# The opening of a graph-network kernel: first input tile in halves, third tile normalised by VectorE, edges turned last, biases fetched first

## The reference

```python
h = jnp.maximum(_layernorm(x, axis=-1), 0.0)
x = x + _L0_gnn_ref(h, edge_index, edge_type_5, ...)   # two chained projections, masked attention of 16 heads, output projection
h = jnp.maximum(_layernorm(x, axis=-1), 0.0)
x = x + _L1_gnn_ref(h, edge_index, edge_type_8, ...)   # mean over the edges of each of 8 relations, then a gate
h = jnp.maximum(_layernorm(x, axis=-1), 0.0)
x = x + _L2_gnn_ref(h, src, dst, ...)                  # two layers of neighbour means
h = jnp.maximum(_layernorm(x, axis=-1), 0.0)
x = x + _L3_gnn_ref(h, edge_weight, ...)               # a sparse weight built from the edges
```

## Time and profile before

| what | value |
|---|---|
| median of 3 runs | 928.15 us (927.82 to 928.22) |
| the profiled execution's own time | 927.87 us |
| its span in the profile | 926.1 us |
| PE busy | 906.8 us, 98% of the span |
| DVE, ACT, POOL busy | 611.5, 359.2, 492.3 us |
| mean granted TensorE clock | 0.996 of full speed |

### The profile page before, as it was taken

How to read it: one execution, slowest core, us unless ns; L and a number is a source line. 1 busy time by engine, 2 the same in 40 slices (tenths; PEclk the granted TensorE clock), 3 DMA queues, 4 the chain that set the end, 5 groups by cost and what they waited for, 6 DMA issues and landing times.

```text
span 926.1 us, 13755 instructions
## 1 busy us (share of the span) xinstructions
PE 906.8 (98%) x4787; PEld 799.0 (86%) x4787; DVE 611.5 (66%) x993; ACT 359.2 (39%) x558; POOL 492.3 (53%) x436
## 2 busy tenths in 40 slices
PE   4999999999999999999999999999999999999998
PEld 4999999998888888888888888888888878888886
DVE  6998888896996735665656565565656565434545
ACT  6433333345885343223223223232325235224422
POOL 5334446775765515757657575756686402220463
PEclk8999999999999999999999999999999999999999
DMA  8998756634336644344554444444333534323412
GB/s 207 241 277 224 229 155 151 167 85 119 53 52 204 178 155 146 92 151 114 152 152 130 153 113 150 113 148 111 97 91 137 182 98 154 114 93 91 140 42 91
DMA packets 89907, 128.60 MB, mean 139 GB/s; under 512 B 34480, under 2 KB 67456, under 8 KB 89856
## 3 DMA queue, kind: packets, MB, share of 16 engines
q1 hardware_dynamic: 72784, 123.54, 43.8%
q0 software_dynamic: 15552, 0.11, 4.0%
q10 hardware_dynamic: 1520, 4.30, 1.4%
HBM read 117.17 MB, written 7.59 MB: 135 GB/s over the span
## 4 chain that ended last, share of the span: by engine, by line
PE 90%; DVE 3%; ACT 2%; POOL 1%; DMA 1%; issue 1%; POOLq 0%; DVEq 0%; ACTq 0%
PE ps L682 49%; PE ps L476 17%; PE ps L756 9%; PE ps L520 4%; PE ps L645 4%; PE ps L600 2%; PE ps L543 2%; PE ps L556 2%; DMA weight_d<-weight_sum,cell 1%; PE ps L435 1%; POOL weight_d L1890 1%; PE ps L892 1%; DVE wlo_all L1388 1%; POOL mean_lo L1869 0%; PE ps L443 0%
## 5 line engine op out<-in xcount | busy, mean ns | idle before, releaser
L1388 DVE TENSOR_TENSOR wlo_all<-raw,whi_all 128x1024 fp32r<-128x1024 f32 x120 | 200.4, 1681 | 119.6 <-ACT whi_all L972 118.5
L476 PE MATMUL ps<-acts,whi_all 128*128 128x384 f32 (+1 forms) x640 | 164.1, 337 | 0.8 <-DVE acts L1400 0.6
L1869 POOL TENSOR_TENSOR mean_lo<-mean_f,mean_hi 128x384 fp32r<-128x384 f32 x76 | 88.3, 1162 | 120.4 <-ACT mean_hi L1124 120.4
L1124 ACT ACTIVATE mean_hi<-mean_f 128x384 fp32r<-128x384 f32 x76 | 39.9, 525 | 277.2 <-DVE mean_f L1562 277.2
L682 PE MATMUL ps<-whi_all,mean_hi 128*128 128x512 f32 x452 | 139.5, 390 | 0.3 <-POOL mean_lo L1869 0.3
L682 PE MATMUL ps<-wlo_all,mean_hi 128*128 128x512 f32 x452 | 139.3, 389 | 0.0
L682 PE MATMUL ps<-whi_all,mean_lo 128*128 128x512 f32 x452 | 139.3, 389 | 0.0
L972 ACT ACTIVATE whi_all<-raw 128x1024 fp32r<-128x1024 f32 x120 | 125.1, 1050 | 32.0 <-PE ps L682 28.5
L476 PEld LDWEIGHTS ps<-acts,whi_all 128*128 128x128 f32 x640 | 116.8, 190 | 1.2 <-DVE acts L1400 0.9
L1890 POOL DMA_INDIRECT weight_d<-weight_sum,cell x48 | 95.5, 1989 | 30.4 <-DMA weight_d<-weight_sum,cell 17.5
L476 PE MATMUL ps<-acts,wlo_all 128*128 128x384 f32 (+1 forms) x320 | 107.6, 336 | 0.0
(11 more groups left out here) (211 smaller groups left out, 1705.6 us busy)
## 6 DMA issues: line engine op xcount, KB each, us to landing
raw<-in_L_gnn_weight SPq DMA_DIRECT2D x64, 512.0 KB
rows_b<-rows_d SPq DMA_DIRECT2D x24, 384.0 KB, 4.8
raw<-in_L_gnn_w_gate SPq DMA_DIRECT2D x16, 512.0 KB
raw<-in_L_gnn_W_self SPq DMA_DIRECT2D x16, 512.0 KB
raw<-in_L_gnn_W_neigh SPq DMA_DIRECT2D x16, 512.0 KB
count_d<-total_r SPq DMA_DIRECT2D x8, 576.0 KB
rel_r<-count_d SPq DMA_DIRECT2D x8, 576.0 KB, 4.5
raw<-in_L_gnn_wq SPq DMA_DIRECT2D x32, 128.0 KB
```

Source lines behind the costliest of these rows:

```text
L476: mm = pe.matmul(ps[:, j % 2, 0:N], stationary[j % RING][:, k, :], acts[:, a, moving, k, :], start=i == 0, stop=i == 3 * KT - 1)
L1124: act.activation(mean_of(q, k, 0)[:, 0, :], sums_of(q, k), ACT.Copy).then_inc(S["mean_hi"], 1)
L1388: dve.tensor_tensor(wlo_row[slot], raw[slot][:, :], whi_row[slot].bitcast(F32), ALU.subtract)\
L1869: pool.tensor_tensor(mean_of(q, k, 1)[:, 0, :], sums_of(q, k), mean_of(q, k, 0)[:, 0, :].bitcast(F32), ALU.subtract).then_inc(S["mean_lo"], 1)
```

## The change

It changes the lists of the opening and nothing behind them.

- SP fetches tile 0 of x in two halves of columns, each with a semaphore, so there is one more DMA ahead of everything else of SP.
- DVE takes the statistics by halves: half 0 of tile 1 now stands before the reciprocal and shift of tile 0, and half 0 of tile 2 before those of tile 1. The edge keys are formed after tile 0 and wait for two of the four edge fetches; the types and the third key come after `start_low(0)`.
- The reciprocal and shift of tile 2 come behind `turn_tile(0, 0)`. DVE then normalises the third tile in two halves (`start_norm`, a multiplication and an addition, with no maximum). ACT takes the maximum while it writes the high part (Relu in place of Copy), DVE while it writes the low part.
- The edges are turned behind all four pieces of x, into other columns of the same bank as the biases. PE no longer waits for their copy; ACT does, before it copies the biases. DVE copies the edges behind `start_low(3)`, and the three softplus operations follow there. Both stand before `turn_tile(0, 1)`.
- POOL fetches the biases right behind the identity, before its tables.

```diff
--- before.py
+++ after.py
@@ -164,7 +164,7 @@
         ps = ctx.enter_context(nc.psum_tensor("ps", [P, 8, 512], F32))
 
 
-        names = """x_in edges_in etw_in bcol_in brow_in out_stored
+        names = """x_in ends_in edges_in etw_in bcol_in brow_in out_stored
             rows_stored mask_based tables_zeroed weights_zeroed mask_in weight_in
             ident_made order_made spare_made zeros_made ones_made mask_base_made
             key_made edge_rows edges_turned edge_cols edges_moved met_made rows_free
@@ -189,6 +189,7 @@
         weights_added = [sem(f"weights_added{q}") for q in range(GROUP)]
         rel_in = [sem(f"rel_in{i}") for i in range(2)]
         x_part = [sem(f"x_part{nt}") for nt in range(NT)]
+        x_half = sem("x_half")
         v_staged = [sem(f"v_staged_{s}") for s in ("even", "odd")]
 
 
@@ -276,7 +277,9 @@
         @block.sync
         def _(sp_):
             x_rows = x.rearrange("(t p) d -> p t d", p=P)
-            for nt in range(NT):
+            sp_.dma_start(xres[:, 0, 0:HALF], x_rows[:, 0, 0:HALF]).then_inc(x_half, 16)
+            sp_.dma_start(xres[:, 0, HALF:D], x_rows[:, 0, HALF:D]).then_inc(x_part[0], 16)
+            for nt in range(1, NT):
                 sp_.dma_start(xres[:, nt, :], x_rows[:, nt, :]).then_inc(x_part[nt], 16)
 
             def key_rows(s):
@@ -423,7 +426,7 @@
             def turn_edges():
                 pe.wait_ge(S["edge_rows"], 1)
                 for f in range(4):
-                    mm = pe.transpose(ps[:, 0, EC * f:EC * f + EC], e_row[:, f, :], ident[0:EC, 0:EC])
+                    mm = pe.transpose(ps[:, 2, P + EC * f:P + EC * f + EC], e_row[:, f, :], ident[0:EC, 0:EC])
                 mm.then_inc(S["edges_turned"], 1)
 
             def turn_two(y, source, f):
@@ -481,17 +484,15 @@
 
             pe.wait_ge(S["ident_made"], 2)
             for n, (nt, k0, k1) in enumerate(START):
-                if n == 2:
-                    turn_edges()
                 pe.wait_ge(S["h_ready"], n + 1)
                 for k in range(k0, k1):
                     mm = pe.transpose(ps[:, 2 + 2 * nt + k // 4, P * (k % 4):P * (k % 4) + P],
                                       h0[:, nt, P * k:P * k + P], ident[:, :])
                 mm.then_inc(S["start_turned"], 1)
+            pe.wait_ge(S["start_lo"], 1)
+            turn_edges()
             pe.wait_ge(S["bcol_in"], 16 * 6)
-            pe.wait_ge(S["start_lo"], 1)
             pe.transpose(ps[:, 2, 0:6 * KT], b_in[:, :], ident[0:6 * KT, 0:6 * KT]).then_inc(S["bcol_made"], 1)
-            pe.wait_ge(S["edge_cols"], 1)
 
             def turned_at(k):
 
@@ -900,7 +901,8 @@
         @block.scalar
         def _(act):
             for f, field in enumerate((src, dst, et8, et5)):
-                act.dma_start(e_in[:, f, :], field.rearrange("(c p) -> c p", p=P)).then_inc(S["edges_in"], 16)
+                act.dma_start(e_in[:, f, :], field.rearrange("(c p) -> c p", p=P))\
+                   .then_inc(S["ends_in" if f < 2 else "edges_in"], 16)
             act.wait_ge(S["ones_made"], 1)
             act.activation(std[:, 0, :], epsc[:, :], ACT.Sqrt).then_inc(S["ones_made"], 1)
             act.dma_start(etw_b[:, :], etw.partition_broadcast(P)).then_inc(S["etw_in"], 16)
@@ -938,8 +940,8 @@
 
                 nt, k0, k1 = START[n]
                 act.wait_ge(S["start_turned"], n + 1)
-                act.activation(acts[:, 0, 0, k0:k1, P * nt:P * nt + P], start_block(nt, k0, k1), ACT.Copy)\
-                   .then_inc(S["start_hi"], 1)
+                act.activation(acts[:, 0, 0, k0:k1, P * nt:P * nt + P], start_block(nt, k0, k1),
+                               ACT.Copy if nt < NT - 1 else ACT.Relu).then_inc(S["start_hi"], 1)
 
             HALVES = [slice(0, HALF), slice(HALF, D)]
 
@@ -980,10 +982,8 @@
             norm_relu_0(*START[0])
             norm_std(0, 1)
             norm_relu_0(*START[1])
+            norm_std(0, 2)
             start_high(0)
-            norm_std(0, 2)
-            norm_relu_0(*START[2])
-            norm_relu_0(*START[3])
             tile_high(0, 0)
             start_high(1)
             start_high(2)
@@ -995,6 +995,7 @@
             act.activation(sp[:, 4, :], sp[:, 3, :], ACT.Ln, bias=1.0).then_inc(S["sp_ln"], 1)
             act.activation(ones_r[:, :], same[:, 0, 0:P], ACT.Copy).then_inc(S["ones_made"], 1)
             act.wait_ge(S["bcol_made"], 1)
+            act.wait_ge(S["edge_cols"], 1)
             act.activation(bcol[:, :], ps[:, 2, 0:6 * KT], ACT.Copy).then_inc(S["bcol_made"], 1)
             act.wait_ge(S["bcol_made"], 2)
 
@@ -1276,28 +1277,44 @@
                 dve.tensor_scalar(shift[:, nt, :], mv[:, nt, 0:1], rstd[:, nt, :], -1.0, ALU.mult, ALU.mult)\
                    .then_inc(S["shift_ready"], 1)
 
-            def start_stats(nt):
-
-                dve.wait_ge(x_part[nt], 16)
-                norm_stats(0, nt)
-
-            for nt in range(NT):
-                start_stats(nt)
-                if nt < NT - 1:
-                    norm_shift(0, nt)
-            dve.wait_ge(S["edges_in"], 16 * 4)
-            dve.scalar_tensor_tensor(e_row[:, KEY, :], e_in[:, 0, :], float(N), e_in[:, 1, :], ALU.mult, ALU.add)\
-               .then_inc(S["key_made"], 1)
-            dve.scalar_tensor_tensor(e_row[:, KEY_T, :], e_in[:, 1, :], float(N), e_in[:, 0, :], ALU.mult, ALU.add)
-            norm_shift(0, NT - 1)
-            dve.tensor_copy(e_row[:, TYPE, :], e_in[:, 3, :])
-            dve.wait_ge(S["key_made"], 1)
-            dve.scalar_tensor_tensor(e_row[:, REL_KEY, :], e_in[:, 2, :], float(N * N), e_row[:, KEY, :],
-                                     ALU.mult, ALU.add).then_inc(S["edge_rows"], 1)
-            dve.wait_ge(S["etw_in"], 16)
-            link(dve.tensor_scalar(sp[:, 0, :], etw_b[:, :], 0.0, None, ALU.max))
-            link(dve.tensor_scalar(sp[:, 1, :], etw_b[:, :], -1.0, None, ALU.mult))
-            dve.tensor_tensor(sp[:, 2, :], etw_b[:, :], sp[:, 1, :], ALU.max).then_inc(S["sp_max"], 1)
+            def edge_keys():
+
+                dve.wait_ge(S["ends_in"], 16 * 2)
+                dve.scalar_tensor_tensor(e_row[:, KEY, :], e_in[:, 0, :], float(N), e_in[:, 1, :], ALU.mult, ALU.add)\
+                   .then_inc(S["key_made"], 1)
+                dve.scalar_tensor_tensor(e_row[:, KEY_T, :], e_in[:, 1, :], float(N), e_in[:, 0, :], ALU.mult, ALU.add)
+
+            def edge_types():
+
+                dve.wait_ge(S["edges_in"], 16 * 2)
+                dve.tensor_copy(e_row[:, TYPE, :], e_in[:, 3, :])
+                dve.wait_ge(S["key_made"], 1)
+                dve.scalar_tensor_tensor(e_row[:, REL_KEY, :], e_in[:, 2, :], float(N * N), e_row[:, KEY, :],
+                                         ALU.mult, ALU.add).then_inc(S["edge_rows"], 1)
+
+            def start_norm(nt, k0, k1):
+
+                dve.wait_ge(S["shift_ready"], nt + 1)
+                dve.tensor_scalar(h0[:, nt, :].rearrange("p (f b i) -> p b f i", f=KT, b=4)[:, :, k0:k1],
+                                  xres[:, nt, :].rearrange("p (b f i) -> p b f i", f=KT, b=4)[:, :, k0:k1],
+                                  rstd[:, nt, :], shift[:, nt, :], ALU.mult, ALU.add).then_inc(S["h_ready"], 1)
+
+            dve.wait_ge(x_half, 16)
+            half_stats(0, 0)
+            dve.wait_ge(x_part[0], 16)
+            half_stats(0, 1)
+            var_of(0, 0)
+            edge_keys()
+            dve.wait_ge(x_part[1], 16)
+            half_stats(1, 0)
+            norm_shift(0, 0)
+            half_stats(1, 1)
+            var_of(0, 1)
+            dve.wait_ge(x_part[2], 16)
+            half_stats(2, 0)
+            norm_shift(0, 1)
+            half_stats(2, 1)
+            var_of(0, 2)
 
             def meet(n):
 
@@ -1352,19 +1369,32 @@
 
                 nt, k0, k1 = START[n]
                 dve.wait_ge(S["start_hi"], n + 1)
-                dve.tensor_tensor(acts[:, 0, 1, k0:k1, P * nt:P * nt + P], start_block(nt, k0, k1),
-                                  acts[:, 0, 0, k0:k1, P * nt:P * nt + P].bitcast(F32), ALU.subtract)\
-                   .then_inc(S["start_lo"], 1)
+                low, high = [acts[:, 0, a, k0:k1, P * nt:P * nt + P] for a in (1, 0)]
+                if nt < NT - 1:
+                    dve.tensor_tensor(low, start_block(nt, k0, k1), high.bitcast(F32), ALU.subtract)\
+                       .then_inc(S["start_lo"], 1)
+                else:
+                    dve.scalar_tensor_tensor(low, start_block(nt, k0, k1), 0.0, high.bitcast(F32), ALU.max,
+                                             ALU.subtract).then_inc(S["start_lo"], 1)
 
             dve.wait_ge(S["h_ready"], 1)
             turn_tile(0, 0)
+            norm_shift(0, 2)
+            start_norm(*START[2])
+            start_norm(*START[3])
             start_low(0)
-            dve.wait_ge(S["edges_turned"], 1)
-            dve.tensor_copy(e_col[:, :, :], ps[:, 0, 0:4 * EC].rearrange("p (f c) -> p f c", f=4))\
-               .then_inc(S["edge_cols"], 1)
```

(19 more changed lines are left out.)

## The result

The kernel after takes 932.22 us (median of 11 runs, 930.0 to 937.36), the kernel before 927.91 on the same chip (11 runs, 927.80 to 928.22). The ratio is 1.0053, interval 1.0038 to 1.0068: slower by about 0.5%, beyond the 0.2% that can be told from no change. The forecast of 928.4 (927.4 to 929.8, "same" at 0.87) was wrong. The profiled execution of after took 932.22 too, against 927.87 of before; its span is 930.5 against 926.1, so 4.4 us are to be found.

A forecast was written before the change was run, and what follows sets the result against it. PE, busy 98%, was bound in the opening by DVE's chain from `turn_tile(0, 1)` to line 1400. That start was 11.4 + 6.79 = 18.2 us against 17.99: +0.2 us, so 928.4 against the median, range 927.4 to 929.8.

The forecast's parts named there:

- when `turn_tile(0, 0)` can start: DVE's first weight-tile turning, waiting for the weight's landing: 11.4 us taken, with 10.4 and 12.3 kept as the ends.
- rival 4: Tile 0's halves save 0.6 us of DVE that the third tile's landing swallows; 928.4 as forecast, no chance of its own.
- types and third key: 0.33: DVE's operations on edge types and third key, between `turn_tile(0, 0)` and `turn_tile(0, 1)`: 0.33 us, from 11.89 - 11.56.
- `start_norm` at 0.32: DVE's normalising of tile 2's halves, 128x512 each: 0.32 us start to start, twice 0.64; 1.20 kept for the range.
- The softplus: Three DVE operations now before `turn_tile(0, 1)`, priced at 0.49 us from 12.38 - 11.89.
- only the start of `turn_tile(0, 1)` counts: Opening chain from DVE's second weight-tile turning to PE at line 1400: 10.58 us unaltered, so its start decides the time.
- the bias wait on PE would go and bring nothing: PE's 3.2 us wait for biases before its first output tiles leaves its chain; line 1400 does not wait for it.
- the biases' new place costs nothing: POOL issues six bias fetches before its tables, which then end some 3.6 us later, at 10.3; priced at nothing.
- DVE's own list would be the bound from `turn_tile(0, 0)` on: DVE's steps up to `turn_tile(0, 1)` have no late wait on another engine: a sum of 6.79 us, 7.35 upper bound.
- Rival 1: Long DVE list: `start_norm` takes one column a cycle (+0.56) or first weight lands at 12.3 (+0.9); 928.9 to 929.9, chance 0.22.
- Rival 2: First weight tile is early, `turn_tile(0, 0)` starts at 10.4: -0.8 us from `turn_tile(0, 1)` on; 927.6 or 927.4, chance 0.13.
- Rival 3: PE waits almost 3 us for line 1400 and its clock falls again: 1.9 us cost, 930.3, chance 0.06.

The follow-up runs named there:

- the variant with 0.65 less: The change with first tile whole, types and third key behind tile 2's statistics, and edges' copy and softplus behind `turn_tile(0, 1)`: 928.55 us, ratio 1.0000.
- biases late: The changed kernel with POOL fetching the six biases behind its tables again, as in the kernel before: 931.19 us, ratio 1.0042.
- types early: The changed kernel with biases behind POOL's tables again, and edge types and third key formed behind tile 2's statistics: 931.21 us, ratio 1.0035.
- halves alone: The kernel before with only x tile 0 fetched in two column halves by SP, statistics taken by halves: 930.67 us, ratio 1.0014.
- 64 rows each: The kernel before with x tile 0 fetched by SP in two fetches of 64 whole rows: 930.65 us, ratio 1.0010.

## Why the prediction was wrong

**The step that failed** is "when `turn_tile(0, 0)` can start": 11.4 taken, 12.3 kept as the upper end, 13.95 measured. I worked out the weight's landing from the bytes that had passed at each time in the kernel before and let the change's order of fetches pass at the same pace, with one issue more. The pace did not stay: with the first tile's fetch divided on SP's queue, us 3 to 5 move 165 to 231 GB/s instead of about 400. That is 2.55 of the missing 3.94 us. It is shown from both sides: taken out of the change (first tile whole), T0 is at 11.45, which is the forecast; put alone into the kernel before, the sag is there. Of the five kernels whose first fetch is divided on SP's queue, all five profiles have x's second tile late (7.4 to 9.5 us; with all of x whole on SP's queue, or the second half on ACT's, it was there by 6.7), and four have the weight late (12.6 to 14.1); none of their 46 executions was below 928.49. The landing that I worked out for the kernel before, 11.2, was right: its trace has the last piece at 11.15. I had read the halves as a gain of 0.6 us that the third tile's landing swallows (rival 4); that a divided first fetch could delay all behind it was in no rival and in no bound.

**The second term mis-sized** is "types and third key: 0.33", measured 1.39. I took it from where it stood, ahead of `turn_tile(0, 0)`, and did not ask what POOL does where it is put: it stands beside POOL's first low part, and DVE's CAST waits until that ends. I had noted when that POOL operation can start (13.6 at the earliest), and only asked whether it would be late, not whom it would hold. The Trainium skill has the rule ("SBUF — State Buffer", "Who interferes with whom"): DVE in its two-port mode and GpSimd take a shared pair of SBUF ports for a whole instruction, and whoever comes second is blocked. The traces agree in eight kernels: beside the low part in four (1.25 to 1.28 us) and beside the operation on the mask in four (0.41 to 0.91), DVE goes on within 0.01 us of the end of POOL's operation, wherever the CAST began. Where no operation of POOL stands beside it the CAST took 0.16 to 0.21. That the ports are the reason is the page's; the runs show only this.

**The third**, `start_norm` at 0.32, measured 0.46 from start to start: between the ends given (0.32 and 0.60), and 0.28 us in all. The softplus cost 0.08 more. The forecast's argument that a one-source operation on fp32 is faster than a two-source one held: 0.54 us long, where the two-source one took 0.68. With these three put in, the list gives 6.79 + 1.06 + 0.28 + 0.08 = 8.21 us, and 8.19 is measured.

**What was right.** That only the start of `turn_tile(0, 1)` counts: 4.15 us there became 4.15 us at PE, and the variant with 0.65 less brought PE on 0.66 sooner. That the bias wait on PE would go and bring nothing, and that the biases' new place costs nothing: 1.0002 for it alone. That DVE's own list would be the bound from `turn_tile(0, 0)` on without idle time: there is none before T1. Rival 1, the long list, came true with another cause than I gave it (the CAST, not `start_norm` alone): by itself, with the first tile whole, it gives 929.59, inside its 928.9 to 929.9. That is luck, since `start_norm` did not take one column a cycle and the weight was not at 12.3 there. (The range's upper end, 929.8, should have been that rival's 929.9.) Rival 2 did not occur. Rival 3, PE's second cold stretch, did not occur in the change, where PE started late as well and waited only 1.0 us; it did in three variants in which DVE or PE came sooner. Its price, 1.9 us forecast, was 1.5 and 1.3 in the two where it was worked out. How long a wait it takes was not found: the clock fell behind waits of 1.7, 1.9 and 2.4 us and not behind two of 1.6. The rule of the Trainium skill that I set against it ("TensorE: Matmul & The Clock Gate", "Part 4: PE-mode transpose": transposes do not count as PE being busy) is spoken against by the pace of transposes before any product has run: in after eight of them, from 16.13, took 1.11 us, where the first eight in before took 1.94. The twelve transposes in a wait, behind which the clock stayed at 1.00, fit that but are one profile.

**What stays open** is why a divided first fetch slows those behind it, and why it does so by different amounts: in us 4 the rate was 165 GB/s (after), 220 (biases late), 293 (types early), 154 (halves alone) and 201 (64 rows each). Ruled out as a necessary cause are the half rows, and as sufficient ones the number of fetches, two halves on one queue later in the list, and one place more ahead of x. The runs with x half a microsecond later (six of twelve at 931 and more), and single runs of the kernel before above 930 in the later measurements, suggest that the opening's transfers can fall into the slow pace by their timing alone; this was not profiled. The mask's path, seen in one profile near 216 us, is another candidate for such runs.

## What to carry to other kernels

Where the opening waits for transfers, the first fetch of a queue is no free place to divide: price the landing of everything behind it as unknown, and if a half is wanted early, give the other half to another queue (the landing came back in both kernels where this was tried, though the time of one of them stayed 0.36% above that of before). For each operation that is moved, look at what the other engines do at its *new* place; a 0.2 us operation of DVE behind a 2.4 us one of POOL cost 1.1 us. And when a chain is shortened that PE waits for, look at how long PE idles: an earlier arrival at the wait can cost in clock what the chain brings.

## What the hardware showed that was not expected

- The same 1.5 MB of x had landed at 11.3 us instead of 8.5 with the first tile in two fetches on one queue; in us 3 and 4 the DMA engines' busy share stayed at 0.92 to 1.15 while the rate fell to 165 GB/s. A row of x of 4 KB took up to 1.6 us in the trace of after and up to 1.2 in that of the kernel with the halves alone; in before none took more than 0.7.
- A DVE operation with one source of 48x128, the CAST, took 0.41 to 1.28 us instead of 0.21 beside a POOL operation, and ended with it in eight profiles; one of two sources took 0.63 instead of 0.23. A wide one of PSUM and SBUF, `start_low(0)`, took 1.22 us beside POOL and 1.21 without it.
- PE's clock was at its lower level for 3.3 us soon after idle times of 1.7, 1.9 and 2.4 us. Behind waits of 0.6 (before), 0.9 and 1.0 (after) it did not fall, and neither did it behind the 1.6 us of the two variants with the biases late and with the first tile whole. With 1.6 on one side and 1.7 on the other, the profiles do not show whether the idle time alone decides.
- Whether PE's first products run at 0.52 or at 0.33 us differs between kernels of nearly the same opening (0.33 in three of the profiles), and a fast start only brings PE to its wait earlier. In five of the profiles those products took 0.52 us while the granted clock was shown as 1.00: there the pace of the products told the clock better than the clock's own column.
- The spread of a kernel's runs grew from 0.4 us to 7 us with the change (927.80 to 928.22 before, 930.0 to 937.36 after, on the same chip). In later measurements the kernel before also had a spread of 5.8 to 7 us.
